# A sparse graph layer on one core: 8 KB runs in the transfers, x and out in blocks of four tiles, and another order of work on GpSimd, TensorE and ScalarE

## What is computed

```python
h = relu(layernorm(x))                       # x: 8192 x 512, fp32
mask = adj > 0                               # adj: 8192 x 8192, fp32
head = mask / max(sqrt(sum(mask * mask, -1)), 1e-12)
inc = adj + head
out = x + (inc @ h) / sum(inc, -1)
```

## Time and profile before

| | us |
|---|---|
| median of 3 runs | 1267.18 (1265.48 to 1268.1) |
| the profiled execution, its own time | 1265.03 |
| its span in the trace | 1263.2 |
| VectorE busy | 1162.8 (92%) |
| ScalarE busy | 977.8 (77%) |
| TensorE busy | 970.4 (77%) |
| DMA, all queues | 471.29 MB, mean 373 GB/s |

### The profile page before, as it was taken

One profiled execution on the slowest core, in us unless ns is written; L12 is line 12 of the kernel. 1 busy time (PEld: TensorE's weight loads), 2 busy tenths in 40 slices (PEclk: granted clock), 3 DMA queues, 4 the chain that ended last, 5 costly groups with the idle time before them and its releaser, 6 DMA issues.

```text
span 1263.2 us, 14630 instructions
## 1 busy us (share of the span) xinstructions
PE 970.4 (77%) x2678; PEld 482.8 (38%) x2678; DVE 1162.8 (92%) x2794; ACT 977.8 (77%) x1903; POOL 764.9 (61%) x745
## 2 busy tenths in 40 slices
PE   0002889988888888888888888798888878878676
PEld 0001334444444434444433444344444434434343
DVE  6679999999999999999998999989999989998972
ACT  6657888898888887888887787788878778876551
POOL 1003666766666667676666666775666667667453
PEclk9999999888889999889988988988899889998698
DMA  9999999999999999999999999999999999999442
GB/s 360 428 421 406 398 402 392 392 394 399 396 391 402 401 399 398 384 401 394 384 398 368 400 398 391 388 395 373 402 400 400 385 382 387 398 399 355 142 143 79
DMA packets 148127, 471.29 MB, mean 373 GB/s; under 512 B 24386, under 2 KB 24386, under 8 KB 143876
## 3 DMA queue, kind: packets, MB, share of 16 engines
q1 hardware_dynamic: 90368, 331.38, 66.9%
q0 software_dynamic: 57664, 138.93, 29.9%
HBM read 490.21 MB, written 33.82 MB: 415 GB/s over the span
## 4 chain that ended last, share of the span: by engine, by line
DVE 45%; DMA 20%; issue 20%; ACT 5%; SPq 5%; another core or an unknown queue 2%; PE 1%; DVEq 0%; ACTq 0%; POOL 0%; POOLq 0%
DMA adj_tile<-in_adj_dram 17%; DVE folded L774 15%; DVE cand_word L779 12%; DVE cand_index L783 5%; DMA gathered_rows<-in_x_dram 3%; SPq L385 2%; ACT junk L569 2%; DVE cand_word L797 2%; SPq L392 2%; DVE cand_index L802 2%; ACT adj_tile L556 2%; SPq L396 1%; DVE ln_stats L757 1%; DVE weights_and_payload L914 1%
## 5 line engine op out<-in xcount | busy, mean ns | idle before, releaser
L488 POOL DMA_INDIRECT gathered_rows<-h_scratch,slot_column x520 | 536.8, 1032 | 265.9 <-issue 161.2
L569 ACT ACTIVATE junk<-adj_tile,zero_unit 128x2048 bf16<-128x2048 f32 x256 | 510.1, 1994 | 111.2 <-issue 75.5
L1330 PE MATMUL acc<-gathered_rows,diag 128*128 128x512 f32 x1040 | 504.1, 641 | 0.5 <-issue 0.5
L488 POOL DMA_INDIRECT gathered_rows<-h_scratch,spill_column x197 | 220.5, 1119 | 199.0 <-ACT spill_column L615 150.8
L774 DVE SCALAR_TENSOR_TENSOR folded<-adj_tile 128x1024 f32<-128x1024 f32 x248 | 301.4, 1215 | 12.1 <-DMA adj_tile<-in_adj_dram 10.7
L1330 PEld LDWEIGHTS acc<-gathered_rows,diag 128*128 128x128 f32 x1040 | 213.7, 212 | 247.1 <-issue 246.8
L779 DVE MAX8 cand_word<-folded 128x8 f32<-128x1024 f32 x248 | 302.9, 1221 | 2.2
L783 DVE FIND_INDEX8 cand_index<-cand_word,folded 128x8 uint32<-128x1024 f32 x248 | 302.2, 1218 | 0.0
L1341 PE MATMUL acc<-gathered_rows,spill_matrix 128*128 128x512 f32 x394 | 186.3, 607 | 14.6 <-issue 10.7
L632 ACT ACTIVATE diag<-ident,weights_and_payload 128x128 f32<-128x128 f32 x582 | 176.2, 387 | 0.5 <-DVE weights_and_payload L914 0.5
L1278 PE MATMUL poff<-spill_rank,lanes_before 128*128 128x1 f32 x130 | 26.4, 272 | 187.5 <-DVE spill_rank L859 174.4
(11 more groups left out here) (146 smaller groups left out, 829.8 us busy)
## 6 DMA issues: line engine op xcount, KB each, us to landing
adj_tile<-in_adj_dram SPq DMA_DIRECT2D x256, 1024.0 KB
h_scratch<-adj_tile SPq DMA_DIRECT2D x16, 1024.0 KB, 10.5
out_dram<-out_tile SPq DMA_DIRECT2D x64, 256.0 KB
gathered_rows<-in_x_dram SPq DMA_DIRECT2D x12, 1024.0 KB, 12.6
x_residual<-in_x_dram SPq DMA_DIRECT2D x48, 256.0 KB
gathered_rows<-h_scratch,slot_column POOLq DMA_INDIRECT x520
x_held<-in_x_dram SPq DMA_DIRECT2D x4, 1024.0 KB, 7.9
gathered_rows<-h_scratch,spill_column POOLq DMA_INDIRECT x197
```

The lines of the kernel that those rows point to most:

```text
L488: nc.gpsimd.indirect_dma_start(out=into, out_offset=None, in_=h[:, :], in_offset=bass.IndirectOffsetOnAxis(ap=column, axis=0), bounds_chec ...
L569: nc.scalar.activation(junk[:, n % 2].rearrange("p (j c) -> p j c", j=2), both[:, :, half], ACT.Relu, bias=zero_unit[:], scale=-UP, accum_ ...
L1330: last = nc.tensor.matmul(acc[t % 3][:], diag[:, t % 2, 1 + s], slot(t % 2, s), start=False, stop=False)
```

## The change

- **Runs of 8 KB.** Chunk j of a tile is now 2048 neighbouring columns, one run of 8 KB a lane. The fold joins columns c and c + 1024 of the chunk. The constants of the columns follow (`diag_chunk`, `base_own`, `base_spill`, `columns_any`).
- **Blocks of four tiles.** Five groups of x are held. The output of tile t is written over its x (`out_of`), so `x_residual` and `out_tile` go. SyncE stores a group of four tiles by 1 MB with runs of 8 KB, and loads a later group of x into the freed place: eleven such loads.
- **GpSimd** gathers the own rows of tile t first, then the spill rows of tile t - 2. The gather of the batch's x moves behind the loop.
- **TensorE** does `residual` and `product_own` right behind `find_owner`, then `offsets`, `bring_spill` and last `product_spill`.
- **A fourth accumulator** (`ptr[0]`) is used up to tile 55.
- **ScalarE** does `row_again` and `own_matrices` ahead of the first check, `copy_owner` ahead of `roots`, and evicts tile t - 5 between the second and third check of period t; from tile 56 on it evicts tile t - 4 behind the fourth.
- **The batch** has four spill groups instead of three, and one VectorE operation of `mark_rows` goes.

```diff
-    HELD_CHUNKS = 4
+    HELD_CHUNKS = 5
+    FOUR = TILES - 8
-    x_t = x.rearrange("(c p j) d -> c j p d", p=P, j=ROWS)
-    out_t = out.rearrange("(c p j) d -> c j p d", p=P, j=ROWS)
-    adj_h = adj.rearrange("(c p j) (h n) -> c j p h n", p=P, j=ROWS, h=2)
+    out_ln = out.rearrange("(c p j) d -> c p j d", p=P, j=ROWS)
+    adj_t = adj.rearrange("(c p j) n -> c j p n", p=P, j=ROWS)
-        held = sb("x_held", [P, HELD, D], fp32)
-        xres = sb("x_residual", [P, 2, D], fp32)
+        held = sb("x_then_out", [P, HELD, D], fp32)
-        osb = sb("out_tile", [P, 2, D], fp32)
         def groups(t):
-            return EXTRA if FOLDED <= t < BATCH else FOLDED_EXTRA
+            return EXTRA if wide(t) else FOLDED_EXTRA
+        def acc_of(t):
+            return (acc + [ptr[0]])[t % 4] if t < FOUR else acc[(t - FOUR) % 3]
+        def late_evicted(t):
+            return t < FOUR
...
-                sp.dma_start(chunk(t % 2, j), adj_h[t // ROWS, t % ROWS, :, :, CW * j:CW * (j + 1)]).then_inc(adj_loaded[t % 2][j], 16)
+                sp.dma_start(A[:, t % 2, 2 * CW * j:2 * CW * (j + 1)],
+                             adj_t[t // ROWS, t % ROWS, :, 2 * CW * j:2 * CW * (j + 1)]).then_inc(adj_loaded[t % 2][j], 16)
+            def load_x(c):
+                sp.wait_ge(out_stored[(c - HELD_CHUNKS) % 2], 16 * ((c - HELD_CHUNKS) // 2 + 1))
+                sp.dma_start(group(c), x_ln[c]).then_inc(x_loaded[c % 2], 16)
+            def store_group(c):
+                sp.wait_ge(out_ready, ROWS * c + ROWS)
+                sp.dma_start(out_ln[c], group(c)).then_inc(out_stored[c % 2], 16)
...
-                if t >= 4:
-                    store_tile(t - 4)
-                if t >= HELD:
-                    load_x(t)
+                if t >= 2 * ROWS and t % ROWS == 1:
+                    store_group(t // ROWS - 2)
+                if t % ROWS == 3 and HELD_CHUNKS <= t // ROWS - 2 + HELD_CHUNKS < LN:
+                    load_x(t // ROWS - 2 + HELD_CHUNKS)
...
@@ GpSimd
-                gather_spill(t - 2)
-                if t < BATCH:
-                    gather_own(t)
+                gather_own(t)
+                if t >= 2:
+                    gather_spill(t - 2)
@@ ScalarE, period
-                check(t, 0)
                 if pay:
-                    own_matrices(q)
                     if not wide(q):
                         row_again(q)
+                    own_matrices(q)
+                check(t, 0)
                 if pick:
                     spill_columns(r)
                     spill_matrix(r)
-                if small:
-                    roots(p)
                 if pay:
                     copy_owner(q)
                 check(t, 1)
+                if small:
+                    roots(p)
+                if f >= 1 and late_evicted(f - 1):
+                    finish_tile(f - 1)
                 check(t, 2)
-                if end:
-                    finish_tile(f)
                 if small:
                     reach_places(p)
                 check(t, 3)
+                if end and not late_evicted(f):
+                    finish_tile(f)
@@ TensorE, period
                 if pay:
                     find_owner(q)
-                if end:
-                    product_spill(f)
                 if pay:
                     residual(q)
+                    product_own(q, 0)
+                    product_own(q, 1)
                 offsets(p)
                 if pay:
                     bring_spill(q)
-                    product_own(q, 0)
-                if pay:
-                    product_own(q, 1)
+                if end:
+                    product_spill(f)
@@ TensorE, batch_period
                 find_owner(w)
-                product_spill(u)
                 residual(w)
                 bring_spill(w)
                 product_own(w, 0)
                 offsets(y)
                 product_own(w, 1)
+                product_spill(u)
```

More of the change, by code:

```diff
@@ L190, in x_of, with group, out_of, x_come @@
         def x_of(t):
-            return held[:, t] if t < HELD else xres[:, t % 2]
-        def x_turn(t):
-            return (t - HELD) // 2 + 1
+            return held[:, t % HELD]
+        def group(c):
+            k = c % HELD_CHUNKS
+            return held[:, ROWS * k:ROWS * (k + 1), :]
+        def out_of(t):
+            return again[:] if t == BATCH else held[:, t % HELD]
+        def x_come(t):
+            c = t // ROWS
+            return x_loaded[c % 2], 16 * ((c - HELD_CHUNKS) // 2 + 1)
         incT = F[:, 0, 0:2 * P].rearrange("p (b c) -> p b c", b=2)
@@ L422, in _ @@
                     load_chunk(t + 2, 3)
-            for t in range(TILES - 4, TILES):
-                store_tile(t)
+            for c in range(LN - 2, LN):
+                store_group(c)
             for b in range(2):
-                sp.wait_ge(out_stored[b], 16 * (TILES // 2))
+                sp.wait_ge(out_stored[b], 16 * (LN // 2))
             sp.wait_ge(list_ready, 1)
@@ L434, in _ @@
                     sp.dma_start(A[:, 0, :], adj[bass.ds(row, P, step=ROWS), :]).then_inc(d_adj, 16)
-                    sp.dma_start(xres[:, 0], x[bass.ds(row, P, step=ROWS), :]).then_inc(d_x, 16)
+                    sp.dma_start(held[:, 0], x[bass.ds(row, P, step=ROWS), :]).then_inc(d_x, 16)
                     for c in range(NCH):
@@ L440, in _ @@
                     sp.wait_ge(d_out, j + 1)
-                    sp.dma_start(out[bass.ds(row, P, step=ROWS), :], osb[:, 0]).then_inc(d_stored, 16)
+                    sp.dma_start(out[bass.ds(row, P, step=ROWS), :], held[:, 1]).then_inc(d_stored, 16)
                     sp.wait_ge(d_stored, j * 16 + 16)
@@ L511, in _ @@
                 pool.wait_ge(h_stored[b], 16 * (LN // 4))
-            gather_own(0)
-            gather_own(1)
-            for t in range(2, BATCH + 1):
+            for t in range(BATCH - 1):
                 if t == BATCH - 2:
@@ L786, in part_columns @@
             def part_columns(t, i):
-                if t == BATCH:
-                    return A[:, 0, CW * part(i):CW * (part(i) + 1)]
-                return chunk(t % 2, part(i) % CHUNKS)[:, part(i) // CHUNKS]
+                return A[:, t % 2, CW * i:CW * (i + 1)]
             def part_values(t, i):
@@ L1322, in residual @@
                     pe.wait_ge(row_ready, t + 1)
-                    nc.tensor.matmul(acc[t % 3][:], diag[:, t % 2, 0], again[:], start=False,
+                    nc.tensor.matmul(acc_of(t)[:], diag[:, t % 2, 0], again[:], start=False,
                                      stop=False).then_inc(row_added, 1)
@@ L1329, in product_own @@
                 for s in range(CHUNKS * g, CHUNKS * (g + 1)):
-                    last = nc.tensor.matmul(acc[t % 3][:], diag[:, t % 2, 1 + s], slot(t % 2, s), start=False, stop=False)
+                    last = nc.tensor.matmul(acc_of(t)[:], diag[:, t % 2, 1 + s], slot(t % 2, s), start=False, stop=False)
                 if g == 1:
```

72 lines of the change are left out of this document (29 added, 43 removed).

## The result

The changed kernel takes 1300.82 us in the median (1299.96 to 1307.92, 4 runs); the kernel before, run beside it, 1267.41 (1265.48 to 1268.1). The ratio is 1.028, with a 95% interval of 1.025 to 1.031: slower, outside the range I gave. The profiled execution took 1299.96 us, its span 1298.2.

A forecast was written before the change was run, and what follows sets the result against it. VectorE was taken as the bound, with 29.0 us of the main loop lost to transfers running behind. Terms of -25 (8 KB runs), -0.7 (first tiles) and 0 summed to -25.7, giving 1242 us, range 1236 to 1268.

The forecast's parts named there:

- What bounds the kernel: Main loop: VectorE sets 16.67 us a tile, and 29.0 us are lost to waits on transfers running behind.
- The waits at the fold: VectorE's 13 waits for adj transfers, 10.7 us before the change; forecast to fall near zero.
- the stalls at the entry: VectorE's four waits on a remote release at L941, 19.1 us; none forecast before the end.
- GpSimd and TensorE: Main-loop period: own gathers and own product first still give `offsets` at 324.6, 1.4 us to spare; cost zero.
- rival D: Gathers fall behind 8 KB packets; rows landing over 8.6 us after issue delay `offsets`; 1298 if one us late; chance 0.16.
- C: Rival: run length isn't what costs, one share of the DMA is slower; pace stays, 1267, no change; chance 0.10.
- Runs of 8 KB, minus 25: Main-loop transfers at 26.4 instead of 24.4 KB per engine and us fall under VectorE's pace; minus 17 to minus 29.
- ScalarE, zero: Same ScalarE instructions in another order, covered by 2.23 us idle ahead of the spill columns; zero.
- Blocks of four, zero: 1 MB x loads and output stores hold up neither SyncE nor the chunks queued behind; nothing on VectorE's path.
- The end, about 0, up to plus 7: Batch and last tiles: fourth group plus 1.8, last store plus 0.5, later spill product minus 2; plus 7 to minus 6.
- B: Rival: the remote stalls at L941 stay, 13 us no longer hidden by VectorE's pace; 1255; chance 0.18.

The follow-up runs named there:

- e13: e6 with TensorE's spill product moved behind `bring_spill`, ahead of the own product, and ScalarE evicting a tile one period older; 1267.0 us, ratio 1.002.
- e17: e13 with x loads and output stores cut to the first tile's rows in each block of four; 1231.9 us, ratio 0.975.
- e9: Changed kernel with TensorE's `offsets` and `bring_spill` ahead of the own product and ScalarE's roots ahead of the spill columns; 1274.7 us, ratio 1.009.
- e2: Changed kernel with adj loaded in runs of 4 KB again, all new orders kept; 1275.9 us, ratio 1.008.
- e15: Kernel before with adj in 8 KB runs and a fourth spill group for the batch, without one `mark_rows` operation; 1272.0 us, ratio 1.005.
- e6: Changed kernel with the old orders on GpSimd, TensorE and ScalarE; 8 KB runs, blocks of four and fourth spill group kept; 1271.4 us, ratio 1.005.
- e7: e6 with adj loaded in runs of 4 KB; 1275.6 us, ratio 1.010.
- e11: Changed kernel with ScalarE's old main-loop order alone, other engines' new orders kept; 1339.9 us, ratio 1.055.

## Why the prediction was wrong

**What bounds the kernel.** Probably right that the main loop lost 29.0 us to transfers: e13, which loses as much (28.8), gets 27.5 of it back when data is taken away (e17). The waits at the fold and the stalls at the entry went as foretold; the time came back elsewhere.

**The step that failed: "GpSimd and TensorE", costed at zero.** It placed the own product ahead of `offsets` by the times at which gathers are issued and `diag` is ready, and took the rows as there. In the period shown the last gather was issued in its tile when I said, but it landed 12.64 us after its issue, where rival D put the limit at 8.6. The 1.4 us to spare were gone, and ScalarE's idle time behind them. `diag` was 2.2 us late as well. 0.8 of that could be read ahead: `row_again` now stands in front of it, and the earlier trace rows show no wait ahead of L632 in which it could hide, so my own working should have given 0.6 us to spare. D's place and mechanism were right; its price, a us in each of 56 periods for each us of lateness, wasn't: the loss by the new orders is 21 to 23 us in the main loop. VectorE waited in `pay_places` 28 times in all (13 and 15 in the rows above), not in every period. That 1300.8 lies near D's 1298 is chance: D added 56 to a gained 1242.

I gave D 0.16, with two arguments against it. "Gathers have their own queue" was no evidence of when a row lands, and the trace of before showed no wait for own rows in an order in which `offsets` did not stand behind them. And the 10.5 us for 1 MB were misread. The row that I took for adj chunks is of the 16 stores of h in the layer norm (L376 alone gives the same 4.9, 10.5 and 13.9); the page gives no landing for the chunks (part 6, before):

```profile
adj_tile<-in_adj_dram SPq DMA_DIRECT2D x256, 1024.0 KB
h_scratch<-adj_tile SPq DMA_DIRECT2D x16, 1024.0 KB, 10.5
```

With that, C's "14 us behind the median" has no median either: for chunks in the main loop only those on the chain are known, 23 to 27 us each.

**Runs of 8 KB, minus 25.** The second step that failed, a term mis-sized. 26.4 KB was read where no gathers ran beside. Beside them it was 25.0, a third of the gain where my lower bound had half, and the mended orders still lose 28.8 and 29.3 us in the main loop (e13, e9) where I had 4 left. On the whole kernel the mended pairs give 1 to 8 us. The term also had nothing for rows made later by longer runs: in the new orders 8 KB costs 25 us (changed against e2), in the old order it costs 0.5% or saves 4.2 us (e15; e6 against e7).

**ScalarE, zero.** Wrong as a statement on its own: its old order beside TensorE's new one costs 33 to 39 us more (e11). It did what the new set needs.

**Blocks of four, zero.** Right for the time with 8 KB runs (e6 and e15 both at 1.005); with 4 KB, blocks and fourth group cost 1.0% (e7).

**The end, about 0, up to plus 7.** It took 12.9 us more. The fourth group, which I had as the main term, isn't it. The longer end goes with the new orders of the last tiles; which of GpSimd and TensorE there, is open.

**Rivals.** B's stalls are gone from the changed kernel's main loop, but chunks in time aren't enough for that: with the old orders and 8 KB runs (e6) VectorE has no wait for adj at the fold and four at the entry, 16.1 us. With less data they are gone as well (e17). So they weren't one thing with the waits for adj, as I had taken them. C is half right: the run length is a small part of what the transfers cost.

## What to carry to other kernels

Before a product that reads gathered rows is moved ahead of a step that others wait for, measure how long a row takes from issue to landing in that stage; that nobody waits for it in the old order tells nothing. A rate read where one queue runs alone can't be carried to the stage in which two share the engines: 26.4 KB per engine and us became 25.0 here. When an order is changed on one of several engines that hand work round in a ring, change and time the whole set: a part of one cost 33 to 145 us here.

## What the hardware showed that I had not expected

The DMA share doesn't tell whether transfers hold a kernel up: it is 0.99 in the changed kernel, which loses 51.5 us in the main loop, and 1.00 in e17, which loses 1.3 (500 to 1100 us; the GB/s, 382 and 385, don't tell them apart either). On the chain of waits a gather of 128 own rows took 7.4 to 13.9 us from issue to landing in the changed kernel and 17 to 20 in e13, though GpSimd issues one each 1.3 us; with 8 KB runs beside it TensorE's waits for them hardly depended on the load (93.5 and 95.2 us). Bytes in 8 KB runs cost 26.4 KB per engine and us alone and 25.0 beside gathers, against 24.4 in shorter runs: the gain of 8% seen alone is 2 to 3% in company.
